# Self-attention in one transformer block: half sums of exponentials added by DMA, one copy of keys and queries, maxima sent on ScalarE's queue

## What is computed

```python
xn = layer_norm(x, ln0_w, ln0_b)
q, k, v = jnp.split(xn @ qkv_w.T, 3, axis=-1)      # then 16 heads of 32
attn = jnp.einsum('bhnd,bhmd->bhnm', q, k) * SCALE  # 2048 x 2048 for each head
attn = jax.nn.softmax(attn, axis=-1)
sa = _merge(jnp.einsum('bhnm,bhmd->bhnd', attn, v)) @ sa_proj_w.T
x = x + sa
```

## Time and profile before

| what | value |
|---|---|
| median of 3 runs | 3913.47 us (3911.08 to 3914.4) |
| the profiled execution | 3913.35 us |
| its span, first to last instruction | 3911.6 us |
| mean granted clock of TensorE | 0.902 |
| the self-attention's part of the span | about 316 to 2168 us |

### The profile page before, as it was taken

The page is one execution under the profiler, slowest core; times in us unless marked ns, Lnnn a source line. Parts: engine busy times, 40 slices in busy tenths (PEclk is TensorE's granted clock), DMA queues, the critical chain, the costliest instruction groups (busy, mean ns, idle before and its releaser), DMA issues. The chain is left out here.

```text
span 3911.6 us, 57974 instructions
## 1 busy us (share of the span) xinstructions
PE 3591.7 (92%) x17160; PEld 2143.7 (55%) x17160; DVE 2221.3 (57%) x3649; ACT 1601.9 (41%) x2855; POOL 1731.8 (44%) x415
## 2 busy tenths in 40 slices
PE   7998999999999999999999499599996859999999
PEld 6884444444444444444443377334332748888887
DVE  4446777777777777778773344345553743222222
ACT  3221666666666666666566233033333331111111
POOL 0001878887888788878888121132233300000000
PEclk9996999999999999999999699555555979999999
DMA  4546132232313132232410434865743662111110
GB/s 168 181 156 155 36 88 50 69 74 59 80 44 87 41 81 63 65 74 53 92 32 9 157 133 168 181 131 123 149 91 107 240 223 88 43 44 43 43 43 22
DMA packets 197952, 370.25 MB, mean 95 GB/s; under 512 B 28706, under 2 KB 53048, under 8 KB 188652
## 3 DMA queue, kind: packets, MB, share of 16 engines
q1 hardware_dynamic: 197868, 369.15, 34.0%
HBM read 248.68 MB, written 119.34 MB: 94 GB/s over the span
## 5 line engine op out<-in xcount | busy, mean ns | idle before, releaser
L1591 DVE TENSOR_REDUCE self_part_max<-self_first 128x1 f32<-128x512 f32 x2048 | 1265.2, 680 | 378.4 <-PE self_first L1472 375.5
L1562 ACT ACTIVATE self_expo<-self_second 128x512 f32<-128x512 f32 x2048 | 1074.2, 602 | 754.6 <-PE self_second L1489 754.6
L1453 POOL TENSOR_TENSOR self_pair_sum<-self_expo 128x2048 f32<-128x2048 f32 x256 | 1170.2, 4576 | 365.6 <-ACT self_expo L1562 365.6
L1472 PE MATMUL self_first<-self_k_move,self_q_hold 96*128 96x512 f32 x2048 | 895.2, 444 | 31.3 <-DVE self_part_max L1591 18.8
L1489 PE MATMUL self_second<-self_q_move,self_k_hold 98*128 (+1 forms) x2048 | 812.4, 400 | 4.3 <-ACT self_expo L1562 4.2
L1472 PEld LDWEIGHTS self_first<-self_k_move,self_q_hold 96*128 96x128 f32 x2048 | 393.9, 193 | 587.7 <-DVE self_part_max L1591 308.9
L1500 PE MATMUL self_weighted<-self_expo,self_v_sb 128*32 128x512 f32 x4096 | 545.5, 604 | 10.0 <-issue 10.0
L1489 PEld LDWEIGHTS self_second<-self_q_move,self_k_hold 98*128 98x128 f32 x2048 | 388.7, 191 | 84.7 <-ACT self_expo L1562 24.8
L1943 DVE CAST mlp_h_high<-mlp_h 128x512 fp32r<-128x512 f32 x128 | 54.7, 427 | 504.6 <-PE mlp_out_sum L61 504.6
L1918 ACT ACTIVATE mlp_h<-mlp_hidden_sum,mlp_b_col 128x512 f32<-128x512 f32 x128 | 88.0, 688 | 601.0 <-PE mlp_hidden_sum L61 601.0
L937 POOL TENSOR_TENSOR cross_pair_sum<-cross_expo 77x2048 f32<-77x2048 f32 x32 | 144.7, 4521 | 358.8 <-ACT cross_expo L1072 358.8
(11 more groups left out here) (163 smaller groups left out, 4187.7 us busy)
## 6 DMA issues: line engine op xcount, KB each, us to landing
self_q_hold<-q_t SPq DMA_DIRECT2D x384, 64.0 KB, 2.1
self_k_move<-k_t SPq DMA_DIRECT2D x96, 256.0 KB
self_q_move<-q_t SPq DMA_DIRECT2D x96, 256.0 KB, 4.5
self_k_hold<-k_t SPq DMA_DIRECT2D x96, 256.0 KB, 4.7
cross_q_hold<-cq_t SPq DMA_DIRECT2D x24, 1024.0 KB, 12.0
cross_q_move<-cq_t SPq DMA_DIRECT2D x24, 1024.0 KB, 14.5
qkv_x<-in_x SPq DMA_DIRECT2D x8, 1024.0 KB, 5.7
v<-qkv_v_sb SPq DMA_DIRECT2D x32, 256.0 KB, 2.0
```

The costliest lines, as they stand in the source:

```text
L1453: nc.gpsimd.tensor_tensor(pair_sum[:, p % pair_slots], expo[:, t % p_slots], expo[:, (t + 1) % p_slots], ALU.add).then_inc(pool_done, 1)
L1472: nc.tensor.matmul(first[:, in_ring[n]], q_hold[0:base, a, s * P:(s + 1) * P], k_move[0:base, a, k0:k0 + TOK], start=True, stop=True).then ...
L1562: nc.scalar.activation(expo[:, t % p_slots, a], second[:, n % ring], ACT.Exp, scale=scale).then_inc(exp_done, 1)
L1591: nc.vector.tensor_reduce(part_max[:, a * SUB + s, k:k + 1], first[:, in_ring[n]], AX_X, ALU.max).then_inc(first_read, 1)
```

## The change

The keys and the queries are held once. `k` has two slots of a group's keys and `q` four slots of a stage's queries; both passes read the same tensors, with their two operands' roles exchanged. The loads into the second copies go. The keys of the next group are loaded in one go at the start of a group's first stage. The loops of PE, ACT and SP now run over rounds of 8 stages.

The sums: pairs 0 and 1 are added by POOL straight into the two halves of `half_sum`. Pairs 2 to 7 go to two buffers of `pair_sum`; the pairs 2 and 4 are added to half 0 and 3, 5 and 6 to half 1 by DMAs that POOL issues and that add to what lies in the destination (`accum_op`). POOL adds pair 7 to half 1 itself. PE sums two groups per stage, half 0 after block 15 and half 1 after block 4 of the next stage. The inverse moves from blocks 3 to 6 to blocks 5 to 8.

The maxima: ACT issues the two DMAs, behind the last exponential of block 13, where SP issued them as soon as its queue came to them.

```diff
-    pair_slots = 4
     pieces = 4
     k_set = n_k // 4
-
-    pool_ops = [("pair", 0), ("pair", 1), ("pair", 2), ("merge", 1), ("pair", 3), ("pair", 4), ("pair", 5), ("merge", 4),
-                ("pair", 6), ("pair", 7)]
-    summed = [0, 1, 3, 4, 6, 7]
-    sum_ready = [pool_ops.index(("merge", p) if ("merge", p) in pool_ops else ("pair", p)) + 1 for p in summed]
-    n_sums = len(summed)
-    sums_after = {1: [(-1, 4)], 2: [(-1, 5)], 8: [(0, 0)], 9: [(0, 1)], 11: [(0, 2)], 15: [(0, 3)]}
-    slot_sum = {0: [0, 3], 1: [1], 2: [4], 3: [2, 5]}
+    q_slots = 4
+    round_stages = 2 * stages_per_group
+    rounds = stages // round_stages
+
+    n_pairs = n_k // 2
+    n_sums = 2
+    n_adds = n_pairs + 1
+    late_sum, early_sum, invert_from, max_sent = 4, 15, 5, 13
...
-        k_move = m.sbuf("k_move", [P, heads, keys], F32R)
-        k_hold = m.sbuf("k_hold", [P, heads, keys], F32R)
-        q_hold = m.sbuf("q_hold", [P, heads, TOK], F32R)
-        q_move = m.sbuf("q_move", [P, 2, heads, TOK], F32R)
+        k = m.sbuf("k", [P, 2, heads, keys], F32R)
+        q = m.sbuf("q", [P, q_slots, heads, TOK], F32R)
         v_sb = m.sbuf("v_sb", [P, n_k, P])
         expo = m.sbuf("expo", [P, p_slots, heads, TOK])
-        pair_sum = m.sbuf("pair_sum", [P, pair_slots, heads, TOK])
+        pair_sum = m.sbuf("pair_sum", [P, 2, heads, TOK])
+        half_sum = m.sbuf("half_sum", [P, 2, heads, TOK])
...
-                def load_max(i):
-                    ge(sp, first_read, reads_until_turned(i), alone=True)
-                    for row, src in ((base, max_high), (base + 1, max_low)):
-                        sp.dma_start(q_move[row:row + 1, i % 2].rearrange("o a (s t) -> o (a s) t", t=P).bitcast(F32),
-                                     src[:].bitcast(F32)).then_inc(max_loaded, 16)
...
+                def add_pair(i, p, to):
+                    t = 2 * p
+                    ge(pool, exp_done, n_seconds * i + heads * (t + 2))
+                    nc.gpsimd.tensor_tensor(to, expo[:, t % p_slots], expo[:, (t + 1) % p_slots], ALU.add).then_inc(
+                        pair_done, 1)
+
+                def add_half(i, p, u, part):
+                    ge(pool, pair_done, n_adds * i + p + 1, alone=True)
+                    pool.dma_start(half_sum[:, u].rearrange("p a t -> p (a t)"),
+                                   pair_sum[:, part].rearrange("p a t -> p (a t)"), accum_op=ALU.add).then_inc(
+                        half_added[u], 16)
 
                 def add_pairs(i):
-                    for at, (what, p) in enumerate(pool_ops):
-                        if what == "pair":
-                            t = 2 * p
-                            ge(pool, exp_done, n_seconds * i + heads * (t + 2))
-                            before = [n for n in slot_sum[p % pair_slots] if summed[n] < p]
-                            if before:
-                                ge(pool, total_done, n_sums * i + before[-1] + 1)
-                            else:
-                                ge(pool, total_done, n_sums * (i - 1) + slot_sum[p % pair_slots][-1] + 1)
-                            nc.gpsimd.tensor_tensor(pair_sum[:, p % pair_slots], expo[:, t % p_slots],
-                                                    expo[:, (t + 1) % p_slots], ALU.add).then_inc(pool_done, 1)
-                        else:
-                            ge(pool, pool_done, len(pool_ops) * i + at)
-                            nc.gpsimd.tensor_tensor(pair_sum[:, p % pair_slots], pair_sum[:, p % pair_slots],
-                                                    pair_sum[:, (p + 1) % pair_slots], ALU.add).then_inc(pool_done, 1)
+                    ge(pool, total_done, n_sums * i - 1)
+                    add_pair(i, 0, half_sum[:, 0])
+                    ge(pool, total_done, n_sums * i)
+                    add_pair(i, 1, half_sum[:, 1])
+                    ge(pool, half_added[1], 48 * i)
+                    add_pair(i, 2, pair_sum[:, 0])
+                    add_half(i, 2, 0, 0)
+                    ge(pool, pair_done, n_adds * i)
+                    add_pair(i, 3, pair_sum[:, 1])
+                    add_half(i, 3, 1, 1)
+                    ge(pool, half_added[0], 32 * i + 16)
+                    add_pair(i, 4, pair_sum[:, 0])
+                    add_half(i, 4, 0, 0)
+                    ge(pool, half_added[1], 48 * i + 16)
+                    add_pair(i, 5, pair_sum[:, 1])
+                    add_half(i, 5, 1, 1)
+                    ge(pool, half_added[0], 32 * i + 32)
+                    add_pair(i, 6, pair_sum[:, 0])
+                    ge(pool, half_added[1], 48 * i + 32, alone=True)
+                    add_half(i, 6, 1, 0)
+                    add_pair(i, 7, pair_sum[:, 1])
+                    ge(pool, half_added[1], 48 * i + 48)
+                    ge(pool, pair_done, n_adds * i + n_pairs)
+                    nc.gpsimd.tensor_tensor(half_sum[:, 1], half_sum[:, 1], pair_sum[:, 1], ALU.add).then_inc(
+                        pair_done, 1)
...
                 def add_up(i, n):
                     if n == 0:
                         ge(pe, mean_done, i)
-                    ge(pe, pool_done, len(pool_ops) * i + sum_ready[n])
+                        ge(pe, half_added[0], 32 * (i + 1))
+                    else:
+                        ge(pe, pair_done, n_adds * (i + 1))
                     for a in range(heads):
                         cols = slice(a * HEAD_DIM, (a + 1) * HEAD_DIM)
-                        mm = nc.tensor.matmul(total[cols], ones[:], pair_sum[:, summed[n] % pair_slots, a],
+                        mm = nc.tensor.matmul(total[cols], ones[:], half_sum[:, n, a],
                                               start=n == 0, stop=n == n_sums - 1)
                     mm.then_inc(total_done, 1)
 
-                def batch(i, j, with_last, with_this):
-                    if j > 0 and with_this:
-                        weigh(i, j - 1)
-                    if j == 0 and with_last:
-                        weigh(i - 1, n_k - 1)
-                    for of, n in sums_after.get(j, ()):
-                        if with_this if of == 0 else with_last:
-                            add_up(i + of, n)
-
...
+                def load_max(r, c):
+                    ge(act, first_read, reads_until_turned(round_stages * r + c), alone=True)
+                    for row, src in ((base, max_high), (base + 1, max_low)):
+                        act.dma_start(q[row:row + 1, c % q_slots].rearrange("o a (s t) -> o (a s) t", t=P).bitcast(F32),
+                                      src[:].bitcast(F32)).then_inc(max_loaded, 16)
 
...
+                        if n == (max_sent + 1) * per_block - 1 and with_next:
+                            load_max(r, c + 1)
...
-                            if with_last and 3 <= j < 3 + pieces and at == 1:
-                                invert(i - 1, j - 3)
-                            if with_last and j == 3 + pieces and at == 1:
+                            if with_last and invert_from <= j < invert_from + pieces and at == 1:
+                                invert(i - 1, j - invert_from)
+                            if with_last and j == invert_from + pieces and at == 1:
                                 divide(i - 1)
 
                 for n in range(n_items):
```

More of the change, by code:

```diff
@@ L1290, in self_phase @@
         exp_done = m.sem("exp_done")
-        pool_done = m.sem("pool_done")
+        pair_done = m.sem("pair_done")
+        half_added = [m.sem(f"half_added{u}") for u in range(2)]
         weighted_done = m.sem("weighted_done")
@@ L1360, in store_out, with load_first_q, period @@
+                def load_first_q(a):
+                    stacked(q[:, 0, a:a + 1], q_t, (0, 1, 0), bass.ds(a * HEAD_DIM, HEAD_DIM), bass.ds(0, TOK),
+                            q_first_loaded[a])
+                def store_out(r, c):
+                    ge(sp, mean_done, round_stages * r + c + 1, alone=True)
+                    group, cols = query_slice(r, c)
                     sp.dma_start(out[bass.ds(group * P, P), cols], mean[:]).then_inc(out_stored, 16)
-                def period(i, g, qt):
+                def period(r, c):
+                    i = round_stages * r + c
@@ L1363, in period @@
                     number = i if isinstance(i, int) else None
-                    has_next = number is None or number < stages - 1
-                    has_after = number is None or number < stages - 2
-                    new_next = (qt + 1) % stages_per_group == 0 and has_next
-                    new_after = (qt + 2) % stages_per_group == 0 and has_after
-                    after = (i + 2) // stages_per_group if number is not None else g + 1
[L1370 to L1375, removed]
@@ L1377, in k_free @@
-                    def k_free(j):
-                        if new_next:
-                            ge(sp, second_done, n_seconds * i + heads * k_set * (j + 1), alone=True)
-                            load_k_hold(g + 1, j)
```

(19 more changed lines are left out.)

176 lines of the change are left out of this document (82 added, 94 removed).

## The result

The changed kernel took 3956.34 us (median of 4, 3953.51 to 3960.9) against 3912.95 for the kernel before (median of 4, 3911.08 to 3914.4): a ratio of 1.0112 [1.0095, 1.013], 43 us slower. I had forecast 3815.

What follows compares the result with a forecast made beforehand. PE was taken to bound the kernel, POOL and DVE next. 3913.35 less 104.6 for removed sums plus 5.6 in the last stage gave 3814.4, say 3815 us; range 3795 to 3950.

Steps and rivals of the forecast that it cites:

- late sum: PE's sum of half 1 after block 4 of the next stage; if POOL is late, PE waits there, all matmuls queued.
- D: Time for an accumulating DMA to land, from its issue: taken as 7.4 us, the middle of 6.5 and 8.3.
- off the path: SP's fewer loads (one copy of keys, one of queries) cost nothing: PE is not short of data in the loop.
- 0.85 us for a sum: PE's cost per group of sums; 123 groups fewer would save 104.6 us if each lies on the path.
- a period of 52.5: PE's new time per stage of the loop: 55.95 less four sums of 0.85, 52.55 us.
- The turn of the maxima: PE turns the maxima after block 11; removing the sum before it costs nothing, without slack up to 26 us.
- the last stage: POOL ends it; one more full add (+4.6 us) and 1 for the chain of landings: +5.6 us.
- The round: POOL's series for half 1: six adds, one issue, three landings, 29.4 + 3D; 51.6 us, deciding from D = 7.7.
- the chain binds a little: Rival: D from 7.7 to 8.85, each us over 7.7 costing 93 us; 3870 us at D = 8.3; chance 0.17.
- The issue, I: POOL's cost to issue one accumulating DMA: taken as 1.0 us, between 0.43 and 4.6.
- ACT's DMAs: ACT issues two DMAs of 0.54 and 0.58 us; taken as costing nothing, 3 us if all 0.1 counted.
- Slower: Rival: D over 8.85 us, POOL's round replaces PE as bound, PE waits after block 4; 4026 to 4110 us; chance 0.19.

Runs made afterwards that it cites:

- e2: Changed kernel, with only the burst of twelve key DMAs waiting for four blocks of the stage: 3896.39 us, 0.9956 of the kernel before.
- e6: Changed kernel, with all query and key loads waiting for three blocks of the stage: 3870.31 us, 0.9888 of the kernel before.
- e7: As e6, with the next group's keys loaded one head per stage instead of in one burst: 3869.62 us, 0.9889 of the kernel before.
- e9: Changed kernel without pair 6's accumulating DMA, that pair left out of the denominators, loads and burst unchanged: 3832.22 us, 0.9787 of the kernel before.
- e10: Changed kernel, with pair 6 added to half 1 by a full-width POOL add instead of a DMA: 3923.76 us, 1.0021 of the kernel before.
- e4: Changed kernel with the sums of the kernel before (six groups of sums, ten POOL adds): 3923.64 us, 1.002 of the kernel before.
- e13: As e7, with PE's and ACT's loops over rounds both written out: 3858.72 us, 0.9851 of the kernel before.

## Why the prediction was wrong

**The step that failed.** I wrote that in a stage with a key burst pair 6's DMA "has some 5 us of slack before the late sum where D is 7.4", and that SP's loads "are off the path". Both are wrong. The slack: from the issue at 1053.77 to PE's turn at 1066.5 are 12.7 us; less 7.4 are 5.3; but the final add of 4.5 lies between landing and sum, so 0.8 was left. I had counted the wait to the sum and not the add. The loads: they are off PE's path, not off the DMA engines that the new chain uses. A landing of 16.7 instead of 7.4 costs the 9.3 over it, less 0.8: 8.5, the wait that the trace shows. To it comes what I had not counted at all, 2.7 us of work at the lower clock behind such a wait. For the loads' price I asked whether PE is short of data, and put at nothing what they do to a DMA that somebody waits for. e2, e6 and e7 move the loads and get the time back; e9 takes away the DMA and gets all of it back. Shown.

**What was right.** 0.85 us for a sum and a period of 52.5 (e9: 52.47). The turn of the maxima cost nothing (a gap of 4.04 us, 3.07 + 0.97), and blocks with a piece of the inverse took 3.19 to 3.21 as before. D alone was right as well: 6.9 at least, 7.9 in the median, 7.4 predicted. A right D didn't help, since I used one D for all 160. The rest adds up: e7, in which the burst no longer matters, is 55 us over the forecast, with 16.5 at the jumps, 16.4 at the late sum, some 12 at block 14 (106.2 against 94.4 before) and 10.9 more in the last stage than I had put there.

**The chain was too close even without loads.** In the last stage SP loads nothing. POOL's timeline of the changed kernel, its last final add last:

```profile
2169.21 0.88 POOL L1407 DMA_DIRECT2D self_half_sum<-self_pair_sum  x1 [0.58 <-POOL self_pair_sum L1402]
...
2178.54 4.56 POOL L1402 TENSOR_TENSOR self_pair_sum<-self_expo 128x2048 f32<-128x2048 f32 x1 [2.26 <-DMA self_half_sum<-self_pair_sum]
2183.68 0.88 POOL L1407 DMA_DIRECT2D self_half_sum<-self_pair_sum  x1 [0.58 <-POOL self_pair_sum L1402]
...
2191.36 0.88 POOL L1407 DMA_DIRECT2D self_half_sum<-self_pair_sum  x1 [2.27 <-DMA self_half_sum<-self_pair_sum]
...
2198.45 4.49 POOL L1435 TENSOR_TENSOR self_half_sum<-self_half_sum,self_pair_sum 128x2048 f32<-128x2048 f32 x1 [1.68 <-DMA self_half_sum<-self_pair_sum]
```

The three landings are 9.3, 7.7 and 7.1 us, 24.1 in all against the 22.2 of 3 x 7.4; the first runs beside two others of POOL's own DMAs, and I had let no DMA of the chain slow another. The round is 53.9 (2144.54, the final add before, to 2198.45), where I had 51.6 and needed 52.55. That is the rival "the chain binds a little", at an average D of 8.0, and it accounts for part of the 33.0 us in stages without a burst (13.6 are left in e6); the query loads at the start of each stage (35.3 in e2 against those 13.6) are the larger part. The first landing is the long one in the loop too: in e7 it is 7.9 us in the median and the other four DMAs of a stage are at 7.1 to 7.2. That the neighbouring DMAs lengthen it was not tested.

**Terms of the wrong size.** The last stage: +16.1, not +5.6. I had put one add and 1 us for landings; e9, with one landing fewer, still needs 56.9 us there against 49.8. The issue, I: 1.5 us with the hand-off and the longer add behind it, not 1.0; harmless with five DMAs, decisive in e10. ACT's DMAs: 9.5 us at block 14, not 0, because the second issue takes 1.37 us in the median; where it takes 0.61, in e4 without POOL's DMAs and in e9 with four of them, block 14 costs only 2 us more than before. The loop of eight stages: 12.1 us and not in my sum at all.

**The rivals.** "Slower" came true in its place (POOL's final add late, PE waiting after block 4), but not by its cause: I had tied it to a D over 8.85 everywhere, and it was some 16 to 17 in six stages and 6.9 to 9.7 in the other 154 landings. I had also written that with D from 6.5 to 8.3 the chain "just fits"; by my own limit of 7.7 it does so only in the lower part. The price of the loads stood under "binds a little", where I had waved it off.

## What to carry to other kernels

When a change puts DMAs in series on a path that somebody waits for, price each landing by what else is in flight at that moment, not by its time alone, and count the slack to the last step before the consumer. When such a chain exists, choose the time of the bulk loads: here the same bytes three blocks later turned 1.1% slower into 1.1% faster. And if the loss is spread over stages, line up the gaps stage by stage: the six bad stages were plain there, and the sums over the whole loop hid them.

## What was not expected of the hardware

- A 1 MB DMA that adds SBUF into SBUF lands in 6.9 us alone and in up to 17.1 beside 3 MB of loads; its issue on POOL takes 0.88 us in the mean (0.87 to 1.07) in either case.
- ACT's second DMA issue, 0.61 us in e4, takes 1.37 us in the median in the changed kernel. That such a DMA is in flight is not enough. In the eleven kernels in which ACT sends the maxima beside such DMAs each of the 207 second issues that began 1.0 to 4.5 us after POOL's own issue took 1.3 us or more; of the 74 that began within 0.5 us of it or over 5.5 us after it, one took more than 1.0. Why is open.
- At the jump of a loop with a long body PE stood for up to 6.2 us on nothing but its own issue (e10), and writing out ACT's loop as well was needed to be rid of all of it. The instruction queue q8 moved 0.82 MB in the kernel before, 2.05 in the changed one and still 1.79 in e13, where the stalls are gone; that fetching instructions is the cause is an inference.
- After a wait of 8.5 us TensorE came back at half its clock: granted 1.00 from 1060 to 1068 us, 0.50 from 1071 to 1082 (PE stood from 1066.5 to 1075.0), 1.00 again from 1085.
